# Attention projections of a two-layer model: one f32 matmul in place of three products of rounded halves

## What is computed

```python
q = norm(x) @ Wq;  k = c @ Wk;  v = c @ Wv        # 16 heads of 64
p = softmax(q k^T / 8 + bias_by_distance + mask)
x = x + tanh(gate) * ((p v) @ Wo)
```

## Time and profile before

| | |
|---|---|
| runs of the kernel | 1568.88 us median of 3, 1566.62 to 1571.58 |
| the profiled execution | 1582.4 us, its span 1579.9 us |
| mean granted clock of TensorE | 0.872 of full speed |
| busy, share of the span | PE 77%, PEld 69%, DVE 59%, ACT 50%, POOL 34% |
| stage `route` | from 171 to 233 us of the span |
| stage `experts` | 233 to about 390 us |
| stage `attend` | 408 to 1088 us |
| stage `moe` | 1088 us to the end |

### The profile page before, as it was taken

The page is one execution under the profiler, slowest core; times in us unless marked ns, Lnnn a source line. Parts: engine busy times, 40 slices in busy tenths (PEclk is TensorE's granted clock), DMA queues, the critical chain, the costliest instruction groups (busy, mean ns, idle before and its releaser), DMA issues. The chain is left out here.

```text
span 1579.9 us, 28066 instructions
## 1 busy us (share of the span) xinstructions
PE 1209.1 (77%) x9252; PEld 1095.7 (69%) x9252; DVE 936.1 (59%) x2025; ACT 785.4 (50%) x2201; POOL 530.2 (34%) x658
## 2 busy tenths in 40 slices
PE   3777217998589999999999999975578767668774
PEld 2555116988578888888888888864577756557773
DVE  4887664453366666568666777774556423223666
ACT  3555213554266667666657555554445434335442
POOL 4333243563000001100164005542225555655541
PEclk8566557999799999999999999996779978888987
DMA  3349744553400000000133003333744555545796
GB/s 97 120 135 264 179 102 130 145 147 76 136 7 14 8 1 21 28 8 1 41 119 110 15 1 122 121 101 130 225 144 135 175 165 157 157 125 166 252 289 222
DMA packets 140545, 181.33 MB, mean 115 GB/s; under 512 B 22496, under 2 KB 120960, under 8 KB 139904
## 3 DMA queue, kind: packets, MB, share of 16 engines
q1 hardware_dynamic: 113040, 127.90, 28.2%
q0 software_dynamic: 17792, 43.14, 8.6%
q10 hardware_dynamic: 9584, 8.60, 1.9%
HBM read 111.51 MB, written 72.32 MB: 116 GB/s over the span
## 5 line engine op out<-in xcount | busy, mean ns | idle before, releaser
L1617 ACT ACTIVATE attend_s<-attend_s,attend_less 128x128 f32<-128x128 f32 x512 | 198.4, 391 | 109.1 <-DVE attend_less L1758 102.5
L2283 POOL DMA_INDIRECT answers<-moe_yb,moe_dst x160 | 158.7, 992 | 166.4 <-ACT moe_yb L2373 128.8
L1572 POOL TENSOR_TENSOR router_xn<-rest_acc,router_mv 128x512 f32<-128x512 f32 x12 | 12.5, 1044 | 445.6 <-DVE router_rs L1234 389.5
L81 PE MATMUL moe_psU<-moe_wh,moe_xl 128*128 (+1 forms) x384 | 119.0, 310 | 0.3 <-issue 0.3
L2429 DVE TENSOR_TENSOR moe_it<-moe_it,moe_psU 128x256 f32<-128x256 f32 x96 | 40.2, 419 | 132.9 <-ACT moe_it L2355 98.8
L82 PE MATMUL moe_psU<-moe_wl,moe_xh 128*128 (+1 forms) x384 | 117.7, 307 | 1.1 <-issue 0.8
L83 PE MATMUL moe_psU<-moe_wh,moe_xh 128*128 (+1 forms) x384 | 117.4, 306 | 0.5 <-issue 0.5
L1635 ACT ACTIVATE attend_pt<-attend_psS 128x1024 f32<-128x1024 f32 x64 | 65.5, 1024 | 95.6 <-PE attend_psS L1909 95.5
L1202 POOL DMA_INDIRECT slots<-router_row,router_idx x80 | 82.0, 1025 | 82.0 <-DMA router_row<-normed_rows 63.0
L2582 PE MATMUL moe_psI<-const_ident,moe_it 128*128 128x128 f32 x192 | 42.2, 305 | 85.0 <-DVE moe_il L2425 79.6
L1756 DVE SCALAR_TENSOR_TENSOR attend_s<-attend_psS,held_bias 128x1024 f32<-128x1024 f32 x64 | 77.9, 1217 | 44.2 <-PE attend_psS L1902 44.1
(11 more groups left out here) (376 smaller groups left out, 4238.5 us busy)
## 6 DMA issues: line engine op xcount, KB each, us to landing
moe_xg<-slots SPq DMA_DIRECT2D x160, 129.0 KB
moe_both<-answers SPq DMA_DIRECT2D x28, 512.0 KB
router_row<-normed_rows SPq DMA_DIRECT2D x40, 256.0 KB
layer_raw<-in_wi_dram SPq DMA_DIRECT2D x8, 1024.0 KB, 5.0
layer_raw<-in_wo_dram SPq DMA_DIRECT2D x8, 1024.0 KB, 7.0
moe_raw<-in_gex_dram SPq DMA_DIRECT2D x17, 384.0 KB, 5.0
moe_both<-normed_rows SPq DMA_DIRECT2D x24, 256.0 KB
slots<-fill SPq DMA_DIRECT2D x32, 129.0 KB
```

Of the source, the lines that this page charges most:

```text
L81: pe.matmul(out, wl, mh, start=first, stop=False)
L1617: last = nc.scalar.activation(s[:, g, j, :], s[:, g, j, :], ACT.Exp, bias=less[:, g, j:j + 1], accum_out=sm[:, g, j:j + 1])
L2283: nc.gpsimd.indirect_dma_start(out=R.YT[q], out_offset=bass.IndirectOffsetOnAxis(ap=dst[:, r % NM, s:s + 1], axis=0), in_=yb[:, r % NY, s, ...
```

## The change

The four projections become plain f32 matmuls, one for each product of three. The weights are loaded by DMA straight into the held tile, in f32, and no high or low part of weights, rows, context or values is made. What ACT wrote as a high part it now writes as a plain f32 copy, and it gives the PSUM bank back itself, where DVE did it before. The order of the units, of the banks and of everything else is as it was. All other layers still use `product`.

```diff
+def whole(pe, out, weights, moving, first, last):
+
+    return pe.matmul(out, weights, moving, start=first, stop=last)
...
-        self.all_high, self.all_low = (m.sb(n, [P, 4 * size], F32R) for n in ("high", "low"))
-        self.high = [self.all_high[:, k * size:(k + 1) * size] for k in range(4)]
-        self.low = [self.all_low[:, k * size:(k + 1) * size] for k in range(4)]
+        self.all = m.sb("weights", [P, 4 * size])
+        self.weights = [self.all[:, k * size:(k + 1) * size] for k in range(4)]
...
         for k, name in enumerate(("Wq", "Wk", "Wv", "Wo")):
-            if k >= 2:
-                sp.wait_ge(self.w_lo, k - 1)
             blocks = PAIRS if name == "Wo" else KD
-            sp.dma_start(self.raw[k % 2][:].rearrange("p (k n) -> p k n", k=blocks), A[name].rearrange("(k p) n -> p k n", p=P)).then_inc(self.raw_in[k % 2], 16)
+            sp.dma_start(self.weights[k].rearrange("p (k n) -> p k n", k=blocks), A[name].rearrange("(k p) n -> p k n", p=P)).then_inc(self.w_in, 16)
...
-        for k in range(4):
-            act.wait_ge(self.raw_in[k % 2], 16 * (k // 2 + 1))
-            self.nc.scalar.activation(self.high[k], self.raw[k % 2][:], ACT.Copy).then_inc(self.w_hi, 1)
...
-        for k in range(4):
-            pool.wait_ge(self.w_hi, k + 1)
-            nc.gpsimd.tensor_tensor(self.low[k], self.raw[k % 2][:], self.high[k], ALU.subtract).then_inc(self.w_lo, 1)
...
-        pool.wait_ge(self.w_lo, 4)
+        pool.wait_ge(self.w_in, 64)
...
-                for u, to, done in [((TURN[0], xh, x_hi), (TURN[1], ch, c_hi))[k] for k in which]:
+                for u, to in [((TURN[0], xt), (TURN[1], ct))[k] for k in which]:
                     used(act, n, u)
-                    nc.scalar.activation(to[:].rearrange("p a b -> p (a b)"), psJ[bank_of(n, u)][:], ACT.Copy).then_inc(done, 1)
+                    nc.scalar.activation(rows(to[:]), psJ[bank_of(n, u)][:], ACT.Copy).then_inc(j_free[bank_of(n, u)], 1)
...
-            def o_high(b, g):
+            def o_out(b, g):
                 act.wait_ge(o_done, unit((b, g)))
-                nc.scalar.activation(oh[:, g * UB:(g + 1) * UB].rearrange("p a b -> p (a b)"), psO[g][:], ACT.Copy).then_inc(o_hi, 1)
+                nc.scalar.activation(rows(o[:, g * UB:(g + 1) * UB]), psO[g][:], ACT.Copy).then_inc(o_up, 1)
...
-            def x_low(n, m, which=(0, 1)):
-
-                for u, high, low, done in [((TURN[0], xh, xl, x_hi), (TURN[1], ch, cl, c_hi))[k] for k in which]:
-                    dve.wait_ge(done, m + 1)
-                    v.tensor_tensor(low[:].rearrange("p a b -> p (a b)"), psJ[bank_of(n, u)][:], high[:].rearrange("p a b -> p (a b)"), ALU.subtract).then_inc(j_free[bank_of(n, u)], 1)
...
-            def o_low(b, g):
-                dve.wait_ge(o_hi, unit((b, g)))
-                r = slice(g * UB, (g + 1) * UB)
-                v.tensor_tensor(ol[:, r].rearrange("p a b -> p (a b)"), psO[g][:], oh[:, r].rearrange("p a b -> p (a b)"), ALU.subtract).then_inc(o_lo, 1)
...
-                            last = product(pe, to[:, j * N:(j + 1) * N], [w[:, k, r] for w in weights], [x[:, k, :] for x in moving], k == 0, k == KD - 1)
+                            last = whole(pe, to[:, j * N:(j + 1) * N], weights[:, k, r], moving[:, k, :], k == 0, k == KD - 1)
...
-                        last = product(pe, to[:], [x[:, k, i * P:(i + 1) * P] for x in (ch, cl)],
-                                       [w[:, k, c * 512:(c + 1) * 512] for w in (wvh, wvl)], k == 0, k == KD - 1)
+                        last = whole(pe, to[:], ct[:, k, i * P:(i + 1) * P], wv[:, k, c * 512:(c + 1) * 512], k == 0, k == KD - 1)
...
-                pe.wait_ge(o_lo, unit((b, 1)))
+                pe.wait_ge(o_up, unit((b, 1)))
                 for m in range(PAIRS):
-                    last = product(pe, to[:, 0:D], (oh[:, m, :], ol[:, m, :]), (woh[:, m, :], wol[:, m, :]), m == 0, m == PAIRS - 1)
+                    last = whole(pe, to[:, 0:D], o[:, m, :], wo[:, m, :], m == 0, m == PAIRS - 1)
```

58 lines of the change are left out of this document (22 added, 36 removed).

## The result

The changed kernel takes **1590.36 us** in the median of its four runs (1583.94 to 1591.5), the kernel before 1567.91 (1566.62 to 1571.58): a ratio of 1.0131, 95% interval 1.0098 to 1.0163. On another chip, with a second profile, it was 1595.29 against 1576.79, ratio 1.0109 (1.0080 to 1.0138). The change makes the kernel slower by 1.1 to 1.3%, some 17 to 21 us. Forecast were 1590 us and slower.

What follows compares the result with a forecast made beforehand. The prediction took TensorE to bound attend nearly alone, DVE pacing each batch's first part and POOL the end of route; attend +34.3 and route -13.3 gave +21 on 1568.9, so 1590 us, range 1576 to 1611.

Steps and rivals of the forecast that it cites:

- Price of a product: TensorE in attend: one plain product takes 0.44 us (256 columns) or 0.88 (512), growing by 0.08 or 0.185.
- Normal step: attend, an even plus an odd batch: 3.2 us longer a step, fifteen steps and the projections together +48 us.
- Late batches: attend, ten batches where DVE is late with router work: relief of DVE gives -15.6 us, bounds 0 and -18.
- Before the first scores: Start of attend: PE gets 4 us more, but DVE's statistics hold the first biased scores almost as long.
- `attend`: Sum for the whole attention stage: 48.2 - 0.6 - 15.6 + 2.3 = +34 us.
- `route`: Routing stage: without POOL's subtractions it ends on Wo's landing at 219.3, -13.3 us, bounds -14 and 0.
- `moe` unchanged: Stage moe: stays as it was, adding nothing to the sum.
- records with the overhead of rounded ones: Rival on attend's matmuls: plain records take 0.48 and 0.93, 5.4 us more a step, 1623 us; chance 0.12.
- That DVE stays as late: Rival on attend: router chains wait on PE and ACT, so 15.6 less comes back, 1606 us; chance 0.10.
- That `route` gives nothing: Rival on the routing stage: the next stage waits for its gathers and loads anyway, 1603 us; chance 0.05.
- Faster through fewer weight loads: Rival on TensorE: weight loads set the pace, two a product instead of three, about 1505 us; chance 0.04.
- Nearly no change: Rival on attend: PE's growth is hidden almost wholly, the stage grows by under 18 us; chance 0.04.

## Why the prediction was right

The sum, term by term, forecast and measured:

- **Price of a product**: 0.44 and 0.88 forecast, 0.43 and 0.86 measured. The step that was mis-sized is the reading of length from the router's 128 columns ("two records of 0.11"): that row, rounded to hundredths, carries up to 5% error. The lower bound, from two records at half clock, was the true one; by it the step would have grown by 2.8 and the sum been some 6 us lower. 24 products in the tail at 0.01 less and 4 at 0.02 less are the 0.3 by which the step came out shorter.
- **Normal step** +3.2 forecast, +2.94 measured; over fifteen steps +48 against +44. That the first block hides its growth (+0.18 forecast in the even batch, 0.16 measured) is confirmed by the kernel with q alone (0.3), and that the tail pays in full by the one with the output projection alone.
- **Late batches** -15.6 forecast, -15.6 measured in the first pair, -14.7 in the means. The size was right, but not its make-up: it was drawn too far towards the subtractions, which give 3.6 over all late batches where PE's slower pace gives 11.1, and it counted the clock in the worst batch alone, where the profile had two more stretches at half clock (from 755.06 and 929.14, 3.4 us each). That the whole came out right is partly luck. The example of a batch that lost 4.4 us was partly one execution's: in the second profile of before that batch took 21.6 us instead of 25.5.
- **Before the first scores**: the prediction let PE's 4 us be hidden almost wholly behind DVE's statistics. They are not: the first scores start 2.5 and 2.9 us later after PE's first matmul in `attend`. But the first even batch then takes 1.1 and 1.8 less (19.0 and 18.3 us instead of 20.1 and 20.0), where the sum had it 0.9 longer. Together this is +1.3 and +1.2 where +0.9 was forecast: the place was wrong, the amount nearly right. At the other end it had +2.3; from the scores of the thirty-first batch to the last output projection the two pairs of profiles give +2.1 and -1.6.
- **`attend`** +34 forecast, +30.5 and +29.5 measured from PE's first matmul in it to the last output projection. Nearly all of the 4 us between them lies in the steps, and so in the price of a product.
- **`route`** -13.3 forecast, -14.8 and -11.9 measured in the two pairs, with Wo's landing as its end (217.8 in the first).
- **`moe` unchanged**: its length wanders by 8 to 10 us from one execution to another, and that, above all, is why the spans of the first two profiles differ by 9 and the runs by 17 to 21.

Measured terms: 30.5 - 14.8 gives +16 in the first pair, 29.5 - 11.9 gives +18 in the second, the runs gave +17 to +21. The median lies on the forecast; a few us of that are luck, since the terms came out a little lower and the expert stage, which the sum left alone, a little longer (+2.9 with the turn to `attend`).

The rivals: records with the overhead of rounded ones are out (0.216 us apart, not 0.24). That DVE stays as late is out for the changed kernel, and a part of it (3.6 us) shows when the subtractions stay. That `route` gives nothing is out. Faster through fewer weight loads is out: PEld fell from 69% to 67% and the kernel became slower. The Trainium skill (Perfetto Trace Analysis, section Identifying the Most-Contended Engine) judges TensorE's headroom by the busy share of weight loads, beside the useful operations as a share of the peak rate. By the share of weight loads the changed kernel would have more headroom; in its trace PE stands still for 6.4 us of the 21 batches instead of 32.4, and the spacing of the matmuls decided. Nearly no change is out for the full change, but it is what happened to q.

## What to carry to other kernels

Cost a longer instruction by the place where it stands: the same 0.07 us a product was almost free in a block paced by another engine (0.16 for sixteen) and paid in full behind it, and the kernel with q alone shows that one projection can be exchanged at no price where all four cost 1%. Lateness that several edits relieve counts once; do not add up gains measured one by one. Look where TensorE's clock falls after a wait: a change that removes the wait gets that back as well. And where a change gains in a side stage, ask whether that gain needs the change: here moving POOL's subtractions and its addition of the bias to DVE and starting two loads earlier gave 0.9% with the old products.

## What the runs showed of the hardware

Plain f32 matmuls run without visible overhead beside the columns: 0.216 us a record for 256 columns and 0.43 for 512, twice as long for twice the columns, while a rounded matmul of 256 columns takes 0.12 and one of 512 0.232. The growth from three rounded matmuls to one plain f32 is thus a factor of 1.20 (256 columns) or 1.24 (512).

Small VectorE operations can last as long as GpSimd's large ones. In before, DVE's addition of 24 elements a partition lasted 4.55 us beside POOL's subtraction; in the second profile of before the neighbours were hit instead:

```profile
216.82 4.63 DVE L703 TENSOR_SCALAR route_f<-route_f,route_nfree,route_free 128x24 f32<-128x24 f32 x1
216.90 8.96 POOL L1047 TENSOR_TENSOR held_low<-making_raw,held_high 128x2048 fp32r<-128x2048 f32 x2 [24.12 <-ACT held_high L1041]
221.48 4.42 DVE L704 TENSOR_TENSOR route_ix<-route_ix,route_f 128x24 f32<-128x24 f32 x1
```

In the changed kernel, with no work on POOL there, the same two take 0.30 and 0.18, and with POOL's subtractions put back into it the first takes 4.38 again, beside a subtraction from 218.11 to 222.60:

```profile
208.99 0.30 DVE L708 TENSOR_SCALAR route_f<-route_f,route_nfree,route_free 128x24 f32<-128x24 f32 x1
209.32 0.18 DVE L709 TENSOR_TENSOR route_ix<-route_ix,route_f 128x24 f32<-128x24 f32 x1
```

```profile
218.26 4.38 DVE L708 TENSOR_SCALAR route_f<-route_f,route_nfree,route_free 128x24 f32<-128x24 f32 x1
```

The Trainium skill (SBUF — State Buffer, section Who interferes with whom) has VectorE and GpSimd share a pair of ports under an exclusive lock, held for a whole instruction; the rows agree in the length, for in each of the four cases DVE's instruction ends within 0.1 us of a POOL subtraction. In the kernel before it cost the stage nothing, since DVE's last instruction of the stage ended at 223.31 and POOL's at 232.62.
